# Layer 0 attention: the scores' 16-row tails ahead of the whole-array products

## The chip, the cores and the metric

The kernel runs on 1 core of one Trainium2 chip. The metric is device time in microseconds (us) of one execution.

## The reference

Two attention layers in sequence, all in float32, on an input of 2 images, 192 channels, 64 x 64 pixels (4096 tokens an image). Only layer 0 matters here:

```python
# --- layer 0 (conv_preact) ---
x = x + _L0_conv_ref(_gn(x), ...)
...
qkv = jnp.einsum('bchw,oc->bohw', x, w_qkv) + b_qkv[None, :, None, None]
qkv = lax.conv_general_dilated(qkv, w_dw, ..., feature_group_count=3 * c) + b_dw[None, :, None, None]
q, k, v = jnp.split(qkv, 3, axis=1)         # 4 heads of 48 channels
q = _l2norm(q, axis=2)
k = _l2norm(k, axis=2)
attn = jnp.einsum('bhdn,bhdm->bhnm', q, k) * temperature[None]
attn = jax.nn.softmax(attn, axis=-1)
out = jnp.einsum('bhnm,bhdm->bhdn', attn, v)
out = jnp.einsum('bchw,oc->bohw', out, w_proj) + b_proj[None, :, None, None]
```

Layer 1 is an attention of its own over the result (one head of 192 channels, 4096 tokens); it follows layer 0 in time and the change does not touch it.

## The kernel before, in words

Layer 0 (function `layer0`) treats 8 heads (4 heads x 2 images) one after the other. A head has 4096 queries and 4096 keys. Its scores are made transposed: a **step** n makes the scores of 128 keys (index m, 32 of them) against 1024 queries (index j, 4 blocks), so a head has 128 steps (`STEPS`) and the layer 1024. The five engines run programs of their own, coupled by semaphores.

What one step needs:

- **Scores, TensorE, lines 637 to 653** (`score`). Queries and keys are each split into a float16 high part and a float16 rest, and the product is high x high + high x rest + rest x high, a contraction over 3 x 48 = 144 rows. 128 of these are stacked in `q_a` and `k_a` and make a whole-array product (line 646), and the last 16 rows, the **tail**, stand in `q_b` and `k_b` and make a second product into the same sums (line 652). A step has two halves of 512 queries, so two whole-array products and two tails, in two PSUM banks. `q_b` and `k_b` hold the tail at the four partition starts 0, 32, 64 and 96, and the four tails of two steps sit in four different groups of 32 rows of the array. Two neighbouring steps have all four banks of `ps_s` between them (`ps_s[:, n % 2]`).
- **Exponential, ScalarE, line 437** (`head`): one instruction reads the 128 x 1024 scores and writes `prob`, of which there are four (`PR`). It waits for `scores` to count both halves of its step and for the weighing that read its `prob` tile last.
- **Weighing, TensorE, line 665** (`weigh`): `prob` (float32) times the values `vt`, whose 64 columns are put on the left or the right half of the array's columns, by half of the queries. The trace has four records for a step, as each float32 product stands there twice.

TensorE's program goes in **pairs of steps**: `score` for the two next steps, then `weigh` for the two steps before. `score` waits on `exped` before it writes into the bank of a step: the exponential of two steps earlier must have read it. The exponentials' semaphore starts at 2.

Behind some pairs the function `prep` puts other work of the next head: **projections** (line 574, float32, 96 x 112, four records each), **sums of squares** (line 588, into 32 columns, eight records) and **transposes** of the values (line 598, four records). In an even head 8 pairs are followed by a projection and two by a set of sums; in an odd head but the last 8 pairs by one projection, two by a set of sums, 4 by two projections each, and 8 by a set of transposes. There are four even heads and four odd heads. Their results go to `ps_h`, which has two banks, and VectorE or ScalarE empties it (VectorE lines 731, 755 and 800 to 802).

Each TensorE wait stands in the order of the program: what is behind it on TensorE waits too. Nothing but the order of the calls sets the order of work. VectorE (the depthwise convolution of the next head, norms, the end of each block), GpSimd and SyncE (the transfers) run beside it and are seldom waited for by TensorE.

Of the kernel before, what the change touches and what calls it, by code (L numbers as in the profile page):

```python
# [17 lines left out]
P = 128  # L18
HALF = 64
KR = HALF + HD  # L20
CH = 512
NCH = N // CH
KT = N // P
NB = 1024
# [8 lines left out]
TAIL = HD - REST  # L33
# [34 lines left out]
def layer0(nc, x, z_dram, w_qkv, vecs, temperature, consts, ss_dram, rn_dram, den_dram, o_dram):  # L68

    with ExitStack() as ctx:  # L70
        def sb(name, shape, dt=F32, scope=None):
            return (scope or ctx).enter_context(nc.sbuf_tensor(name, shape, dt))

        def psum(name, shape):
            return ctx.enter_context(nc.psum_tensor(name, shape, F32))

        def sem(name):
            return ctx.enter_context(nc.semaphore(name))
# [21 lines left out]
        q_a = sb("q_a", [P, 2, N], F16)  # L100
        k_a = sb("k_a", [P, 2, N], F16)
        q_b = sb("q_b", [P, 2, N // 2], F16)
# [37 lines left out]
        ps_s = psum("ps_s", [P, 2, NB])  # L140
# [21 lines left out]
        scores = sem("scores")  # L162
# [38 lines left out]
        with nc.Block() as block:  # L201
# [356 lines left out]
            def _(pe):  # L558
# [64 lines left out]
                for c in range(FAR, 8):  # L623
                    at = c - FAR
                    for tap in range(TAPS):
# [3 lines left out]
                                        start=(tap == 0), stop=(tap == TAPS - 1))  # L629
# [7 lines left out]
                def score(slot, g, a):  # L637
                    if a == 0:
                        for c in range(2):
                            pe.wait_ge(split_in[c], MOVES * 2 * (g + 1))  # L640
                    for n in (a, a + 1):
                        j, m = n // KT, n % KT
                        pe.wait_ge(exped, STEPS * g + n + 1)
                        for h in range(2):
                            cols = slice(j * NB + h * CH, j * NB + (h + 1) * CH)
                            pe.matmul(ps_s[:, n % 2, h * CH:(h + 1) * CH], k_a[:, slot, m * P:(m + 1) * P],  # L646
                                      q_a[:, slot, cols], start=True, stop=False)
                    for n in (a, a + 1):
                        j, m = n // KT, n % KT
                        for h in range(2):  # L650
                            r = REST * (2 * (n % 2) + h)
                            pe.matmul(ps_s[:, n % 2, h * CH:(h + 1) * CH], k_b[r:r + TAIL, slot, m * P:(m + 1) * P],  # L652
                                      q_b[r:r + TAIL, slot, j * CH:(j + 1) * CH], start=False, stop=True).then_inc(scores, 1)

                def head(slot, g, base, prep, pairs_moved=None, last=False):

                    uses = Uses(base)

                    def weigh(a):
                        j, m = a // KT, a % KT  # L660
                        pe.wait_ge(exped, STEPS * g + a + 3)
                        if m == 0:
                            pe.wait_ge(acc_free, NBL * g + j + 1)
                        for h in range(2):
                            ins = pe.matmul(ps_a[h * HALF:(h + 1) * HALF, j % 2, :], vt[:, slot, m, :],  # L665
                                            prob[:, a % PR, h * CH:(h + 1) * CH], start=(m == 0), stop=(m == KT - 1))
                        ins.then_inc(pv_done, 1)

                    for a in range(0, STEPS, 2):
                        if a + 2 < STEPS:  # L670
                            score(slot, g, a + 2)
                        elif not last:
                            score(1 - slot, g + 1, 0)
                        if a == 0:
                            pe.wait_ge(help_free, base)
                            if pairs_moved is not None:
                                pe.wait_ge(vt_moved, pairs_moved)
                        weigh(a)
                        weigh(a + 1)
                        for n in (a, a + 1):  # L680
                            j, m = n // KT, n % KT
                            prep(j, m, uses)
# [30 lines left out]

                pe.wait_ge(help_free, USE_FIRST)
                score(0, 0, 0)
                with pe.Fori(0, PAIRS - 1) as i:
                    even(i)
# [1340 lines left out]
```

## Time and profile before

| | us |
|---|---|
| median of 3 runs | 3410.62 |
| lowest and highest run | 3407.66, 3412.9 |
| the profiled execution, its own time | 3413.54 |
| its span | 3411.8 |
| TensorE matmul busy | 3197.9 (94%) |
| ScalarE busy | 2204.5 (65%) |
| VectorE busy | 1903.0 (56%) |
| GpSimd busy | 934.1 (27%) |

Times in the rows are microseconds from the start of the span, unless marked ns. PE is TensorE's matmul, PEld its weight load (which overlaps PE), ACT is ScalarE, DVE VectorE, POOL GpSimd, SP SyncE. A row of the timeline is a group of neighbouring instructions of one engine and line: start of the first, time from the first start to the last end, engine, line, operation, tiles written and read with their shapes, xcount, and in brackets the idle time of the engine ahead of it with what ended it. The end of a matmul is modelled by the profiler, so starts are the safer reading: a whole-array product of 512 columns is shown as 0.38 us long, while the next one starts 0.22 us after it. A window shows each group only with those of its instructions that touch the window, so a narrow window singles out one instruction.

### The profile page before, as it was taken

Reading aid. Unit: us, or ns where it says so; the run is one execution under the profiler, and the core shown is the slowest. Engines: PE = TensorE matmul, PEld = TensorE weight load, DVE = VectorE, ACT = ScalarE, POOL = GpSimd, SP = SyncE. Lnnn points to the kernel's source line nnn. Section 1 sums busy time; section 2 is a strip of 40 time slices with the busy share of each in tenths; the row PEclk is TensorE's granted clock in tenths of the full one; section 3 lists DMA queues with packets and bytes.
Section 4 is the critical chain, followed back from the end, with each engine's and each line's share of the span. In section 5 each row is a group of like instructions: output and inputs, shape, how many; then the busy total and the mean of one; then the engine's idle time right before and its main releaser. Section 6 shows DMA issues by size and latency. Waiting matters only on the chain. (4 is left out here: it accounts for less than half of the span.)

```text
span 3411.8 us, 47896 instructions
## 1 busy us (share of the span) xinstructions
PE 3197.9 (94%) x16354; PEld 1276.1 (37%) x16354; DVE 1903.0 (56%) x2461; ACT 2204.5 (65%) x2428; POOL 934.1 (27%) x485
## 2 busy tenths in 40 slices
PE   3799999999999999999999778999999787999998
PEld 1222222322223222222222234555555344555555
DVE  6551347431553525375111165888888555888886
ACT  5256556566555665565666524988888256888886
POOL 1002021020020210210200001666666213666665
PEclk7799999999999999999999979999999888999999
DMA  5312113111132021210200042677777824777777
GB/s 151 85 33 61 46 34 72 45 38 50 32 84 54 14 60 43 60 49 26 58 11 10 18 121 81 123 143 144 143 144 143 142 90 100 143 142 142 142 142 134
DMA packets 685382, 286.20 MB, mean 84 GB/s; under 512 B 602416, under 2 KB 644144, under 8 KB 682608
## 3 DMA queue, kind: packets, MB, share of 16 engines
q1 hardware_dynamic: 680400, 275.65, 38.0%
q10 hardware_dynamic: 4800, 8.26, 1.1%
q8 instruction: 97, 1.59, 0.2%
q14 instruction: 85, 0.70, 0.1%
HBM read 85.99 MB, written 34.21 MB: 35 GB/s over the span
## 5 line engine op out<-in xcount | busy, mean ns | idle before, releaser
L437 ACT ACTIVATE prob<-ps_s,cur 128x1024 f32<-128x1024 f32 x1024 | 1085.4, 1111 | 723.1 <-PE ps_s L652 722.0
L665 PE MATMUL ps_a<-prob,vt 128*64 128x512 f32 x4096 | 993.3, 606 | 0.0
L1623 PE MATMUL ps_s<-kst,qs 128*128 128x512 f16 x2560 | 640.4, 383 | 29.4 <-DMA qs<-q_scratch 18.8
L1319 POOL TENSOR_TENSOR p_lo<-gp,p_hi 128x1024 f16<-128x1024 f32 x256 | 550.6, 2161 | 399.6 <-ACT p_hi L1453 394.5
L1636 PE MATMUL ps_o<-v_hl,at_hi 128*128 128x384 f16 x2048 | 548.6, 329 | 33.6 <-DMA at_lo<-p_lo 33.3
L646 PE MATMUL ps_s<-q_a,k_a 128*128 128x512 f16 x2048 | 534.7, 383 | 4.2 <-issue 2.2
L1636 PE MATMUL ps_o<-v_hl,at_lo 128*128 128x192 f16 x2048 | 505.5, 248 | 0.0
L665 PEld LDWEIGHTS ps_a<-prob,vt 128*64 128x64 f32 x4096 | 248.7, 136 | 409.7 <-issue 409.0
L1890 DVE TENSOR_SCALAR_CACHE_REDUCE neg<-ps_s,mix 128x1024 f32<-128x1024 f32 x256 | 327.3, 1278 | 132.5 <-PE ps_s L1623 131.3
L1623 PEld LDWEIGHTS ps_s<-kst,qs 128*128 128x128 f16 x2560 | 245.1, 99 | 257.1 <-issue 31.4
L646 PEld LDWEIGHTS ps_s<-q_a,k_a 128*128 128x128 f16 x2048 | 132.5, 97 | 543.4 <-ACT prob L437 471.4
L405 POOL TENSOR_TENSOR sq<-qk 112x1024 f32<-112x1024 f32 x28 | 52.1, 1894 | 963.3 <-DVE qk L748 963.3
L1435 ACT ACTIVATE gp<-neg,nbias 128x1024 f32<-128x1024 f32 x256 | 290.1, 1133 | 0.0
L1636 PEld LDWEIGHTS ps_o<-v_hl,at_hi 128*128 128x128 f16 x2048 | 201.6, 98 | 201.2 <-DMA at_lo<-p_lo 44.9
L823 DVE RECIPROCAL rden<-rden 128x512 f32<-128x512 f32 x32 | 107.3, 3353 | 299.3 <-DMA rden<-den_scratch 299.3
L748 DVE SCALAR_TENSOR_TENSOR qk<-pad,vec,qk 112x2048 f32<-112x2048 f32 x112 | 254.0, 2346 | 0.0
L1636 PEld LDWEIGHTS ps_o<-v_hl,at_lo 128*128 128x128 f16 x2048 | 201.8, 99 | 51.1 <-issue 1.3
L1926 DVE SCALAR_TENSOR_TENSOR gp<-gp,coef,vb 128x1024 f32<-128x1024 f32 x128 | 209.2, 1675 | 7.2 <-DVE neg L1890 2.6
L1926 DVE SCALAR_TENSOR_TENSOR gp<-gp,coef,rn 128x1024 f32<-128x1024 f32 x128 | 207.5, 1663 | 5.8 <-DVE neg L1890 2.3
L731 DVE TENSOR_SCALAR pad<-ps_h,vec 112x512 f32<-112x512 f32 x80 | 60.1, 752 | 264.1 <-PE ps_h L574 264.0
L652 PE MATMUL ps_s<-q_b,k_b 16*128 16x512 f16 x2048 | 202.4, 385 | 0.0
L1419 ACT ACTIVATE vb<-neg 128x1024 f32<-128x1024 f32 x128 | 134.2, 1048 | 84.9 <-DVE neg L1890 84.7
(226 smaller groups left out, 2728.9 us busy)
## 6 DMA issues: line engine op xcount, KB each, us to landing
z<-z_scratch SPq DMA_DIRECT2D x80, 384.0 KB, 3.8
sq<-rn_scratch SPq DMA_DIRECT2D x14, 768.0 KB, 10.8
qs<-q_scratch SPq DMA_DIRECT2D x64, 128.0 KB, 2.8
rden<-den_scratch SPq DMA_DIRECT2D x64, 96.0 KB, 2.2
o_scratch<-o_s SPq DMA_DIRECT2D x64, 96.0 KB, 1.9
res_scratch<-xg SPq DMA_DIRECT2D x4, 1536.0 KB, 7.3
q_scratch<-qst SPq DMA_DIRECT2D x32, 192.0 KB, 2.4
res<-res_scratch SPq DMA_DIRECT2D x64, 96.0 KB, 2.2
```

The source lines that it names most:

```text
L437: act.activation(prob[:, a % PR, :], ps_s[:, a % 2, :], ACT.Exp, bias=cur[:, slot:slot + 1], scale=1.0 / SPLIT).then_inc(exped, 1)
L646: pe.matmul(ps_s[:, n % 2, h * CH:(h + 1) * CH], k_a[:, slot, m * P:(m + 1) * P], q_a[:, slot, cols], start=True, stop=False)
L652: pe.matmul(ps_s[:, n % 2, h * CH:(h + 1) * CH], k_b[r:r + TAIL, slot, m * P:(m + 1) * P], q_b[r:r + TAIL, slot, j * CH:(j + 1) * CH], sta ...
L665: ins = pe.matmul(ps_a[h * HALF:(h + 1) * HALF, j % 2, :], vt[:, slot, m, :], prob[:, a % PR, h * CH:(h + 1) * CH], start=(m == 0), stop=( ...
L748: ins = dve.scalar_tensor_tensor(out=out, in0=src, scalar=vec[0:KR, slot, 1 + tap:2 + tap], in1=out, op0=ALU.mult, op1=ALU.add)
L1319: pool.tensor_tensor(p_lo[:, cols], prob[s][:, cols], p_hi[:, cols], ALU.subtract).then_inc(lo_made[c], 1)
L1419: act.activation(sqr[s][:, cols], neg[:, c, :], ACT.Relu, scale=-1.0).then_inc(relued[c], 1)
L1435: act.activation(prob[s][:, c * QB:(c + 1) * QB], neg[:, c, :], ACT.Exp, bias=nbias[:, s, c:c + 1], scale=-1.0, accum_out=sums[:, s, c:c + ...
L1623: ins = pe.matmul(ps_s[:, c % 2, h * CH:(h + 1) * CH], qs[:, s, qt, :], kst[:, ktile, cols], start=(t == 0), stop=(t == len(terms) - 1))
L1636: ins = pe.matmul(ps_o[:, s * CH:s * CH + wide], a[:, s, kt, :], v_hl[:, kt, 0:wide], start=(kt == 0 and t == 0), stop=(kt == KT - 1 and t ...
L1890: dve.tensor_scalar(neg[:, c, :], ps_s[:, c % 2, :], mix[:, 6:7], None, ALU.mult, ALU.min, accum_out=nbias[:, s, c:c + 1]).then_inc(mx_op, 1)
L1926: dve.scalar_tensor_tensor(out=prob[s][:, cols], in0=prob[s][:, cols], scalar=coef[:, s, c:c + 1], in1=sqr[s][:, cols], op0=ALU.mult, op1= ...
```

## The change

In `score`, both waits on `exped` of the pair come first. Then come the four tails of the pair, which now begin the sums (`start=True`); then the four whole-array products, which complete them (`stop=True`) and each count up `scores`. Numbers of instructions, operands and the rest of the program stay. Lines behind 641 shift by one: the tails are at line 647, the whole-array products at 653, the weighing at 666, the projections stay at 574.

```diff
                     for n in (a, a + 1):
-                        j, m = n // KT, n % KT
                         pe.wait_ge(exped, STEPS * g + n + 1)
-                        for h in range(2):
-                            cols = slice(j * NB + h * CH, j * NB + (h + 1) * CH)
-                            pe.matmul(ps_s[:, n % 2, h * CH:(h + 1) * CH], k_a[:, slot, m * P:(m + 1) * P],
-                                      q_a[:, slot, cols], start=True, stop=False)
                     for n in (a, a + 1):
                         j, m = n // KT, n % KT
                         for h in range(2):
                             r = REST * (2 * (n % 2) + h)
                             pe.matmul(ps_s[:, n % 2, h * CH:(h + 1) * CH], k_b[r:r + TAIL, slot, m * P:(m + 1) * P],
-                                      q_b[r:r + TAIL, slot, j * CH:(j + 1) * CH], start=False, stop=True).then_inc(scores, 1)
+                                      q_b[r:r + TAIL, slot, j * CH:(j + 1) * CH], start=True, stop=False)
+                    for n in (a, a + 1):
+                        j, m = n // KT, n % KT
+                        for h in range(2):
+                            cols = slice(j * NB + h * CH, j * NB + (h + 1) * CH)
+                            pe.matmul(ps_s[:, n % 2, h * CH:(h + 1) * CH], k_a[:, slot, m * P:(m + 1) * P],
+                                      q_a[:, slot, cols], start=False, stop=True).then_inc(scores, 1)
```

TensorE, a regular pair near the start of the first even head, before (what an instruction waits for is in brackets; a float32 product is one row here):

```order
L643 REGISTER_ALU
L646 MATMUL ps_s<-q_a,k_a 128x512 [waits exped]
L646 MATMUL ps_s<-q_a,k_a 128x512
L643 REGISTER_ALU
L646 MATMUL ps_s<-q_a,k_a 128x512 [waits exped]
L646 MATMUL ps_s<-q_a,k_a 128x512
L652 MATMUL ps_s<-q_b,k_b 128x512 x4
L665 MATMUL ps_a<-prob,vt 64x512 [waits exped]
L665 MATMUL ps_a<-prob,vt 64x512
L665 MATMUL ps_a<-prob,vt 64x512 [waits exped]
L665 MATMUL ps_a<-prob,vt 64x512
```

The same pair now:

```order
L642 REGISTER_ALU
L642 REGISTER_ALU [waits exped]
L647 MATMUL ps_s<-q_b,k_b 128x512 [waits exped]
L647 MATMUL ps_s<-q_b,k_b 128x512 x3
L653 MATMUL ps_s<-q_a,k_a 128x512 x4
L666 MATMUL ps_a<-prob,vt 64x512 [waits exped]
L666 MATMUL ps_a<-prob,vt 64x512
L666 MATMUL ps_a<-prob,vt 64x512 [waits exped]
L666 MATMUL ps_a<-prob,vt 64x512
```

The tails moved from behind the whole-array products to ahead of them, and the second wait on `exped` from between the products to ahead of all.

TensorE, the end of a pair that a projection follows and the start of the next, in the same head, before:

```order
L665 MATMUL ps_a<-prob,vt 64x512 [waits exped]
L665 MATMUL ps_a<-prob,vt 64x512
L574 MATMUL ps_h<-z,w 112x512 [waits z_in1,help_free]
L574 MATMUL ps_h<-z,w 112x512
L643 REGISTER_ALU
L646 MATMUL ps_s<-q_a,k_a 128x512 [waits exped]
L646 MATMUL ps_s<-q_a,k_a 128x512
```

And now:

```order
L666 MATMUL ps_a<-prob,vt 64x512 [waits exped]
L666 MATMUL ps_a<-prob,vt 64x512
L574 MATMUL ps_h<-z,w 112x512 [waits z_in1,help_free]
L574 MATMUL ps_h<-z,w 112x512
L642 REGISTER_ALU
L642 REGISTER_ALU [waits exped]
L647 MATMUL ps_s<-q_b,k_b 128x512 [waits exped]
L647 MATMUL ps_s<-q_b,k_b 128x512 x3
```

Behind the projection's two products stood a whole-array product; now a tail stands there.

## Rows read from the trace of the kernel before

**Rows 1.** The page: TensorE's busy tenths in 40 slices of the span.

```profile
PE   3799999999999999999999778999999787999998
```

**Rows 2.** Windows by stage: attention of layer 0, layer 1.

```profile
core 0: us, PE busy (x) PEld busy (x) DVE busy (x) ACT busy (x) POOL busy (x), PEclk, DMA share, GB/s
145.00:1945.00 1800.00, 1794.40 (x8720) 494.33 (x8720) 705.05 (x533) 1085.43 (x1024) 210.24 (x63) 1.00 0.18 43
1945.00:3411.80 1466.80, 1328.93 (x7460) 750.23 (x7460) 1099.46 (x1820) 1060.19 (x1341) 715.08 (x406) 0.95 0.65 130
```

**Rows 3.** Timeline of one regular pair and the start of the next.

```profile
700.88 0.40 PE L652 MATMUL ps_s<-q_b,k_b 16*128 16x512 f16 x4
701.21 1.94 PE L665 MATMUL ps_a<-prob,vt 128*64 128x512 f32 x8
701.34 2.12 ACT L437 ACTIVATE prob<-ps_s,cur 128x1024 f32<-128x1024 f32 x2 [1.05 <-PE ps_s L652]
...
702.12 0.14 PEld L665 LDWEIGHTS ps_a<-prob,vt 128*64 128x64 f32 x2 [0.28 <-issue]
703.08 1.04 PE L646 MATMUL ps_s<-q_a,k_a 128*128 128x512 f16 x4
703.51 0.11 PEld L646 LDWEIGHTS ps_s<-q_a,k_a 128*128 128x128 f16 x2 [0.32 <-ACT prob L437]
704.05 0.10 PEld L652 LDWEIGHTS ps_s<-q_b,k_b 16*128 16x128 f16 x4 [0.42 <-issue]
704.05 0.39 PE L652 MATMUL ps_s<-q_b,k_b 16*128 16x512 f16 x4
```

**Rows 4.** Timeline, first and last start of a run of 98 regular pairs.

```profile
1629.10 0.39 PE L646 MATMUL ps_s<-q_a,k_a 128*128 128x512 f16 x1
...
1939.69 0.39 PE L646 MATMUL ps_s<-q_a,k_a 128*128 128x512 f16 x1
```

**Rows 5.** Timeline, a regular pair that follows transposes, start to next start.

```profile
609.45 1.03 PE L646 MATMUL ps_s<-q_a,k_a 128*128 128x512 f16 x4 [1.00 <-issue]
...
612.61 0.39 PE L646 MATMUL ps_s<-q_a,k_a 128*128 128x512 f16 x1
```

**Rows 6.** Timeline, the last whole-array product and last two weighing records of a pair.

```profile
700.57 0.38 PE L646 MATMUL ps_s<-q_a,k_a 128*128 128x512 f16 x1
...
702.55 0.60 PE L665 MATMUL ps_a<-prob,vt 128*64 128x512 f32 x2
```

**Rows 7.** Timeline in layer 1: a product's last part and its reader.

```profile
2201.20 0.38 PE L1623 MATMUL ps_s<-kst,qs 128*128 128x512 f16 x1
...
2201.62 1.28 DVE L1890 TENSOR_SCALAR_CACHE_REDUCE neg<-ps_s,mix 128x1024 f32<-128x1024 f32 x1 [0.59 <-PE ps_s L1623]
```

**Rows 8.** Timeline, pairs with a projection and with transposes.

```profile
184.93 1.03 PE L646 MATMUL ps_s<-q_a,k_a 128*128 128x512 f16 x4
...
187.55 0.60 PE L665 MATMUL ps_a<-prob,vt 128*64 128x512 f32 x2
188.08 1.97 PE L574 MATMUL ps_h<-z,w 96*112 96x512 f32 x4
...
189.46 0.59 PE L574 MATMUL ps_h<-z,w 96*112 96x512 f32 x1
189.89 1.03 PE L646 MATMUL ps_s<-q_a,k_a 128*128 128x512 f16 x4
...
604.25 0.60 PE L598 MATMUL ps_h<-ident,vv 112*128 112x112 f32 x4
604.59 0.26 PE L598 MATMUL ps_h<-ident,vv 112*128 112x112 f32 x1
604.68 0.38 PE L646 MATMUL ps_s<-q_a,k_a 128*128 128x512 f16 x1
...
607.84 0.60 PE L598 MATMUL ps_h<-ident,vv 112*128 112x112 f32 x4
```

**Rows 9.** Windows: eight pairs with transposes.

```profile
579.10:609.44 30.34, 29.00 (x162) 10.45 (x160) 10.62 (x21) 17.34 (x17) 0.00 (x0) 1.00 0.05 15
```

## The prediction

> **What bounds the kernel now.** I read the busy times by stage first. The change touches only the attention loop of layer 0, from 145 to 1945 us [rows 2]: TensorE is busy for 1794.4 of 1800 us at a granted clock of 1.00, that is 2.4 GHz, while ScalarE is busy for 1085 us. The page shows the same as a row of nines for PE [rows 1]. So a time can only change there by what TensorE's own sequence costs or by a wait put into it. Busy TensorE is modelled, however, so the order of starts has to be read.
>
> The timeline of one regular pair of steps [rows 3] gives it. Call the four whole-array products S, the four 16-row tails T, the value products V (eight records). Start to start: S to T 0.97, T to V 0.33, V to S 1.87, together 3.17 us. ScalarE in the same rows: two exponentials, 2.12 us, then 1.05 us idle until T has completed both score tiles. 2.12 + 1.05 is also 3.17. That is no accident: the third S's weights are loaded at 703.51, 0.05 us after the second exponential ends (701.34 + 2.12 = 703.46), 0.2 us later than they could be. Two rounds run side by side, TensorE's own and the one through ScalarE, and both last about 3.17 us.
>
> Which is longer? In a run of 98 regular pairs [rows 4] the period is (1939.69 - 1629.10)/98 = 3.169 us. A regular pair that follows other work, where the exponentials were long done, takes 612.61 - 609.45 = 3.16 [rows 5]. So the round through ScalarE binds by some 0.005 to 0.01 us, and TensorE's own round is the floor right below it.
>
> **What the change does to TensorE's own round.** The order S T V becomes T S V, with the same 16 records. What could change is the price of the boundaries. The last S starts at 700.57, T at 700.88 [rows 6]: 0.31, where one S follows another after 0.65/3 = 0.217 (four S busy 1.03, one 0.38 [rows 5, 6]). That is 0.095 extra. From the last V at 702.55 to S at 703.08 is 0.53, where V follows V after 0.43 (702.12 and 702.55, loads and products [rows 3, 6]): 0.10 extra. T to V is 0.33: T's 0.217, 0.01 over its four starts and 0.10. So each of the three changes of array shape costs nearly the same, and a regular pair has three of them in either order. The new round is then T to S 0.33, S to V 0.96 or 0.97, V to T 1.87: 3.165 us, as now without the ScalarE round.
>
> **What it does to the round through ScalarE.** Now the wait for the second exponential stands before T, and the first exponential needs only the first two S. From the end of the exponentials: 0.05 to T's load [rows 3], 0.33 to the first S, 0.23 to the second (rather than 0.217, as its load comes late after a boundary), and from that start to ScalarE's. A whole-array fp16 product releases its reader 0.42 after its start: 2201.20 to 2201.62 on VectorE [rows 7]. Tails need 0.45 (last of four at 700.89, ScalarE at 701.34 [rows 3]). Take 0.42, which is the same form of product: 0.05 + 0.33 + 0.23 + 0.42 + 2.12 = 3.15 us. This is 0.015 below TensorE's own 3.165, so TensorE binds alone. Per regular pair 3.169 falls to 3.165. There are 405 of them (511 pairs with both parts, less the 106 that carry other work, below): **-1.6 us**. Bounds: 3.16 gives -3.6, 3.17 gives +0.4.
>
> **The pairs with other work.** After V, 56 pairs hold one projection, 12 hold two, 24 hold a set of transposes and 14 a set of sums of squares (by the code: 32 + 24 single projections in even and odd heads, 12 double in three odd heads). Now a projection's last record at 189.46 is followed by S at 189.89 [rows 8]: 0.43, which is its own cadence, with no extra. A transpose at 604.59 is followed by S at 604.68, the same 0.09 us by which its predecessors follow each other, again no extra. These use the whole array in width, as S does, so nothing switches. V before the projection does pay: 187.55 to 188.08, 0.53. In the new order T follows the projection or transpose, so that boundary becomes one like S to T, and T to S adds the next. Such a pair goes from three priced boundaries to four. 92 pairs x 0.095 = **+8.7 us** (0.09 to 0.10: 8.3 to 9.2). Their S group also loses its smooth start (1.04 after a boundary [rows 3], 1.03 after a projection [rows 8]): 92 x 0.01 = **+0.9** (0 to 0.9). The 14 sums are 32 columns wide and pay on both sides either way: 0.
>
> No row of before has a projection followed by tails; the price above is taken from S to T. The Trainium skill, TensorEngine Tiling (Array Packing), Key Properties, says that changing the tiling mode, not just the tile, drains the engine. By it projection to S is free and projection to T is not, as in the sum, and it speaks against this change; rows 8 agree for the free half.
>
> Some of that is absorbed. Eight transpose pairs take 30.34 us [rows 9], 3.79 each, while an undisturbed one takes 607.84 - 604.25 = 3.59 [rows 8]; TensorE waits there for VectorE to empty the two helper banks. A longer boundary in front of such a wait shortens it. I take three pairs in each of three heads, 9 x 0.1 = **-0.9** (0 to -2.4, all 24).
>
> Nothing else moves. V's waits are for exponentials of the pair just awaited before T. Behind the merged wait stand S, V and the other work; S lost a head start of two products, which is what the floor of 3.165 counts. The ring of four prob tiles is freed by V of the pair before, done by then. VectorE, SyncE and GpSimd get the same instructions; layer 1 (1467 us) is untouched.
>
> **Sum:** 8.7 + 0.9 - 1.6 - 0.9 = +7.1 us, with ends +2.3 and +10.5. The profiled execution took 3413.54 us (span 3411.8), so 3420.6 by its own time; it lies 2.9 above the median of the runs, 3410.62, so the forecast is 3417.7. Its own range with the scatter of the runs (3407.66 to 3412.9) is 3411 to 3423. What a measurement of this kernel can tell from no change is about 0.2%, 6.8 us; the forecast sits on that edge.
>
> **Rivals.** (a) The round through ScalarE binds. It has only 0.015 us of room. Should a score tile be released as late as tails release it (0.45), it is 3.18; should T have to wait for its weight loads (0.10 for four [rows 3]) after the exponential, 3.25. Each 0.01 over 3.165 costs 4 us in 405 pairs: 3.18 to 3.25 is +6 to +34 on top, 3424 to 3452. Against: products start 0.01 after their load starts in all rows. Chance 0.13.
> On that release the Trainium skill, TensorE: Matmul & The Clock Gate (The cost: per-tile semaphore tail), states that increments of packed matmuls serialize at about 26 ns each. By it the whole-array products release earlier than the second tail did; rows 3 and 7 agree with 0.03 between 0.45 and 0.42, and it makes (a) less likely.
> (b) The other side: T to S costs no drain. This boundary is never seen in the trace. TensorE's round would be 3.07 and ScalarE's 3.05, so 405 x 0.10 = 40 us are gained, 14 sums pairs add 1, and the 92 pairs come out even: 3369. It decides as soon as the boundary costs under 0.07. Against: all three kinds of boundary seen cost 0.095 to 0.10. Chance 0.07. By the skill's rule on the tiling mode, above, it would not happen.
> (c) Projection to T costs nothing, as to S, because only V with its halves makes the array drain at that place. Then -1.6 and little else: 3409, no change. Against: S to T pays. Chance 0.08.
>
> **How the numbers follow.** The forecast has 0.72. Its centre, +7.1, is just over the bound of 6.8, so I give 0.38 of it to slower, 0.33 to no change and 0.01 to faster. With (a) slower, (c) no change, (b) faster: slower 0.51, same 0.41, faster 0.08. The range takes the forecast's own, (c), and the nearer part of (a), and leaves out (b) and the rest of (a): 3409 to 3430.
>
> **What would show it.** Right: V to T 0.53, T to S 0.31 from the last T, S to V 0.31; last projection record to T 0.53 instead of 0.43; periods in the 98-pair run 3.16 to 3.17; ScalarE idle some 1.04 per pair, its first exponential starting before the last S ends. Projection pairs 5.06 instead of 189.89 - 184.93 = 4.96 us [rows 8]. Wrong: V to T over 0.55 in regular pairs with ScalarE named as releaser (rival a), T to S 0.22 (b), projection to T 0.43 (c).

## The result, and the profile after

| | before | changed |
|---|---|---|
| median of the runs, us | 3410.7 (5 runs) | 3427.51 (5 runs) |
| lowest run, us | 3407.66 | 3425.66 |
| profiled execution: own time, us | 3413.54 | 3431.69 |
| its span, us | 3411.8 | 3429.9 |

One of the five runs of the changed kernel was disturbed (10419 us) and the ratio leaves it out; the median of the other four is 3426.93 us, 16.2 above the kernel before. The change makes the kernel slower: ratio 1.0048, 95% interval 1.0034 to 1.0062. The forecast was 3417.7 with a range of 3409 to 3430, and slower as the likeliest sign. The sign and the range hold; of the +16.2 us only +7.1 had been forecast.

The windows of the changed kernel, from its first to its last score product and over layer 1. The columns are those of [rows 2]:

```profile
143.99:1952.80 1808.81, 1804.49 (x8697) 524.41 (x8698) 704.51 (x531) 1082.39 (x1022) 210.11 (x63) 1.00 0.18 43
1957.20:3429.90 1472.70, 1335.75 (x7464) 751.15 (x7460) 1101.92 (x1820) 1060.64 (x1341) 713.31 (x406) 0.95 0.64 129
```

And of the kernel before, from its first to its last score product:

```profile
145.25:1939.69 1794.44, 1789.45 (x8696) 492.95 (x8696) 704.54 (x531) 1082.93 (x1022) 210.24 (x63) 1.00 0.18 43
```

The attention loop is 1808.8 - 1794.4 = 14.4 us longer, at the same granted clock of 1.00. Layer 1, whose program is the same, took between 1467 and 1473 us in the profiled executions of this study, so its difference here (1472.7 against 1466.8 [rows 2]) is the scatter of the measurement and not an effect.

Now the loop at rest. The timeline of a regular pair of the changed kernel in an even head, which answers to [rows 3] (tails are L647, products L653, weighing L666):

```profile
200.57 0.10 PEld L647 LDWEIGHTS ps_s<-q_b,k_b 16*128 16x128 f16 x4 [0.81 <-ACT prob L437]
200.58 0.40 PE L647 MATMUL ps_s<-q_b,k_b 16*128 16x512 f16 x4
200.91 1.04 PE L653 MATMUL ps_s<-q_a,k_a 128*128 128x512 f16 x4
201.55 2.12 ACT L437 ACTIVATE prob<-ps_s,cur 128x1024 f32<-128x1024 f32 x2 [1.04 <-PE ps_s L653]
201.87 1.94 PE L666 MATMUL ps_a<-prob,vt 128*64 128x512 f32 x8
203.74 0.10 PEld L647 LDWEIGHTS ps_s<-q_b,k_b 16*128 16x128 f16 x4 [0.81 <-ACT prob L437]
203.74 0.40 PE L647 MATMUL ps_s<-q_b,k_b 16*128 16x512 f16 x4
```

T to S 0.33, S to V 0.96, V to T 1.87: 3.16 us, as worked out. The exponentials end at 201.55 + 2.12 = 203.67, and the tails' weights are loaded at 203.74, 0.07 after that where a load that waits comes after 0.05: TensorE binds, with 0.02 us of room. Over a run of 25 such pairs it is (1038.73 - 959.62)/25 = 3.164:

```profile
959.62 0.40 PE L647 MATMUL ps_s<-q_b,k_b 16*128 16x512 f16 x4
...
1038.73 0.39 PE L647 MATMUL ps_s<-q_b,k_b 16*128 16x512 f16 x2
```

The pairs with a projection, which answer to [rows 8], last (194.25 - 184.12)/2 = 5.065 us in place of 4.96:

```profile
184.12 0.40 PE L647 MATMUL ps_s<-q_b,k_b 16*128 16x512 f16 x4
...
187.28 1.97 PE L574 MATMUL ps_h<-z,w 96*112 96x512 f32 x4
189.18 0.40 PE L647 MATMUL ps_s<-q_b,k_b 16*128 16x512 f16 x4
...
194.25 0.40 PE L647 MATMUL ps_s<-q_b,k_b 16*128 16x512 f16 x4
```

What was not forecast stands at the end of the loop. The same views of the changed kernel in the last two heads:

```profile
1649.47 2.12 ACT L437 ACTIVATE prob<-ps_s,cur 128x1024 f32<-128x1024 f32 x2 [1.12 <-PE ps_s L653]
1649.80 1.94 PE L666 MATMUL ps_a<-prob,vt 128*64 128x512 f32 x8
...
1651.14 0.60 PE L666 MATMUL ps_a<-prob,vt 128*64 128x512 f32 x2
1651.71 0.13 PEld L647 LDWEIGHTS ps_s<-q_b,k_b 16*128 16x128 f16 x4 [0.85 <-ACT prob L437]
1651.74 0.40 PE L647 MATMUL ps_s<-q_b,k_b 16*128 16x512 f16 x4
```

V to T (last two records at 1651.14, tails at 1651.74) is 0.60 in place of 0.53, and ScalarE is idle 1.12 in place of 1.04. The run of 98 pairs there, the counterpart of [rows 4], has (1952.80 - 1635.56)/98 = 3.237 us a pair:

```profile
1635.56 0.39 PE L647 MATMUL ps_s<-q_b,k_b 16*128 16x512 f16 x4
...
1952.80 0.40 PE L647 MATMUL ps_s<-q_b,k_b 16*128 16x512 f16 x4
```

Six of the eight heads run in a hardware loop (`pe.Fori`), the last two are written out behind it, as the kernel's `even(PAIRS - 1)` and `odd(PAIRS - 1, True)` say. What differs is in the view of the line that waits. For line 642 of the changed kernel it lists what TensorE's sequencer (PEldq) runs: operation, count, shortest, median and longest in ns, first and last start in us:

```profile
L642 PEldq ALU_OP  x759: 32/32/39, 146.8 to 1523.1; - x190
L642 PEldq EVENT_SEMAPHORE  x130: 51/51/51, 142.2 to 1952.7; - x130
```

Before, on its line 643:

```profile
L643 PEldq ALU_OP  x759: 32/32/39, 149.0 to 1519.4; - x190
L643 PEldq EVENT_SEMAPHORE  x2: 51/51/51, 143.7 to 1739.4; - x2
```

In the loop the number of a step is in a register, so each wait has a register instruction ahead of it (the last of the 759 is at 1523), and the first of the two waits rides on the second of these. In the last two heads the numbers are constants, there is no register instruction, and a pair's two waits meet in front of one weight load. There are 128 more instructions that only wait, 51 ns each. The same view for a narrow window shows the one of the pair above:

```profile
L642 PEldq EVENT_SEMAPHORE  x1: 51/51/51, 1651.6 to 1651.6; - x1
```

It starts at 1651.63 in the trace, 0.04 after the second exponential has ended (1651.59), and the tails' load comes 0.08 after that start. In 127 of the 130 the start is 0.04 after the end of the second exponential of a pair. So the later wait is the one that the separate instruction holds.

### The profile page after: what moved, and what is told of

Same layout as the page of the kernel before. It is cut to its first block and busy times, and to the rows that moved or that the text cites. A ratio compares the mean times of both kernels' runs of the same rounds, so it can differ in the third digit from the quotient of the medians.

```text
span 3429.9 us, 48023 instructions
## 1 busy us (share of the span) xinstructions
PE 3218.7 (94%) x16354; PEld 1308.3 (38%) x16354; DVE 1905.2 (56%) x2461; ACT 2204.0 (64%) x2428; POOL 932.2 (27%) x485
## 5 line engine op out<-in xcount | busy, mean ns | idle before, releaser
L666 PE MATMUL ps_a<-prob,vt 128*64 128x512 f32 x4096 | 993.5, 606 | 0.0
L653 PE MATMUL ps_s<-q_a,k_a 128*128 128x512 f16 x2048 | 532.9, 383 | 0.0
L666 PEld LDWEIGHTS ps_a<-prob,vt 128*64 128x64 f32 x4096 | 249.1, 136 | 510.4 <-issue 508.5
L653 PEld LDWEIGHTS ps_s<-q_a,k_a 128*128 128x128 f16 x2048 | 158.8, 98 | 237.7 <-issue 117.2
L647 PEld LDWEIGHTS ps_s<-q_b,k_b 16*128 16x128 f16 x2048 | 55.3, 91 | 407.0 <-ACT prob L437 334.3
L647 PE MATMUL ps_s<-q_b,k_b 16*128 16x512 f16 x2048 | 203.1, 385 | 4.5 <-ACT prob L437 1.9
```

## Experiments

Every version was timed beside the kernel before on the same chip; the ratios are to that kernel. Its medians beside them were 3413.1 us (one wait, waits apart, other work ahead, both edits), 3412.16 (old order with a doubled wait, with one wait, with the other work ahead of the weighing) and 3411.43 (old order with the other work between products and tails, and both edits once more). Two theories stood: **W**, that two waits in front of one instruction cost an instruction on the path from the exponential to the tails, in the last two heads; **D**, that each change of the array's shape costs 0.095 us. The rival to W was that the round through ScalarE is too long there for a reason of its own.

### One wait instead of two

```diff
-                    for n in (a, a + 1):
-                        pe.wait_ge(exped, STEPS * g + n + 1)
+                    pe.wait_ge(exped, STEPS * g + a + 2)
```

> The changed kernel, but the pair waits once on exped, for its second step; the first wait is implied by it. Theory W: in the last two heads, which are written out outside the loop, the two waits in front of the tails become an instruction of its own on TensorE (EVENT_SEMAPHORE L642 in the trace), and it puts 0.07 us into each of about 125 pairs. Then this version takes 3427.5 - 8.7 = 3419 us, V to T is 0.525 everywhere, and no semaphore row stands before the tails. Rival R: the round through ScalarE binds in those heads for a reason of its own (release, bank, ScalarE), whatever the form of the wait. Then it stays at 3427 us with V to T at 0.59 in the last two heads.

3419.35 us, ratio 1.0019 (1.0010 to 1.0028). The run of 98 pairs is back at (1943.84 - 1633.62)/98 = 3.165 us:

```profile
1633.62 0.39 PE L646 MATMUL ps_s<-q_b,k_b 16*128 16x512 f16 x3
...
1943.84 0.40 PE L646 MATMUL ps_s<-q_b,k_b 16*128 16x512 f16 x4
```

and the line that waits has two semaphore instructions left:

```profile
L641 PEldq EVENT_SEMAPHORE  x2: 51/51/51, 141.2 to 1744.3; - x2
```

W stands and the rival falls: ScalarE, the banks and the release are the same in this version. The loop, from its first to its last score product, is 1808.8 - 1801.0 = 7.8 us shorter than in the changed kernel; the ratios (1.0048 and 1.0019) are 0.0029 apart, some 10 us. It is also the kernel that the prediction had costed, and it is 6.2 us above the kernel before where the sum said 7.1.

### The two waits apart

```diff
-                    for n in (a, a + 1):
-                        pe.wait_ge(exped, STEPS * g + n + 1)
                     for n in (a, a + 1):
                         j, m = n // KT, n % KT
+                        pe.wait_ge(exped, STEPS * g + n + 1)
                         for h in range(2):
                             r = REST * (2 * (n % 2) + h)
```

> The changed kernel, with each wait in front of the two tails of its own step, so that no instruction carries two of them. Theory W: as with one wait, 3419 us, with V to T 0.525; the first two tails start early only where ScalarE is late, which is nowhere. Rival R: 3427 us. If the semaphore instruction came from the number of waits of the program, not from two on one instruction, it would be in this trace too.

3417.36 us, ratio 1.0014 (1.0005 to 1.0023). Both waits are there, each on the load of its own tails, and the semaphore instructions are 2 again:

```profile
L643 PEldq EVENT_SEMAPHORE  x2: 51/51/51, 142.5 to 1743.6; - x2
```

So it is not the number of waits but their meeting on one instruction.

### The kernel before with a doubled wait

```diff
                         j, m = n // KT, n % KT
+                        if not (isinstance(g, int) and g == 0 and n == 0):
+                            pe.wait_ge(exped, STEPS * g + n)
                         pe.wait_ge(exped, STEPS * g + n + 1)
                         for h in range(2):
                             cols = slice(j * NB + h * CH, j * NB + (h + 1) * CH)
```

> The kernel before, with a second, weaker wait on exped in front of each whole-array product group; nothing else. Theory W: in the loop the added wait rides on the register instruction and costs nothing; in the last two heads it is an instruction of its own behind the end of the second exponential, in front of the third product: 0.07 to 0.09 us in about 125 pairs, +9 to +11 us, 3420 us, the third product over 0.216 behind the second there. Rival R: the changed kernel's loss has to do with the tails coming first, and this version stays at 3411 us.

3420.46 us, ratio 1.0025 (1.0016 to 1.0034), 8.3 us above the kernel before. The price is paid with the tails last as well. The four products are 1.12 us from first start to last end in place of 1.04 [rows 3], since the third one's load comes late, and ScalarE is idle 1.12 in place of 1.05:

```profile
1641.14 1.12 PE L648 MATMUL ps_s<-q_a,k_a 128*128 128x512 f16 x4
1641.63 0.13 PEld L648 LDWEIGHTS ps_s<-q_a,k_a 128*128 128x128 f16 x2 [0.38 <-ACT prob L437]
...
1642.64 2.12 ACT L437 ACTIVATE prob<-ps_s,cur 128x1024 f32<-128x1024 f32 x2 [1.12 <-PE ps_s L654]
```

The exponentials ahead end at 1639.40 + 2.12 = 1641.52, so the load comes 0.11 after them where it came 0.05 after them before. Its semaphore line (L645 in this version) is:

```profile
L645 PEldq EVENT_SEMAPHORE  x256: 51/51/51, 140.8 to 1943.2; - x128
```

Half of these 256 stand ahead of the first product of a pair. Their exponential has ended some 0.6 us before that product's load, so they hold nothing up.

### The other work ahead of the weighing, in the new order

```diff
-                        weigh(a)
-                        weigh(a + 1)
                         for n in (a, a + 1):
                             j, m = n // KT, n % KT
                             prep(j, m, uses)
+                        weigh(a)
+                        weigh(a + 1)
```

> The changed kernel, both waits kept, but projections, sums and transposes stand between the scores and the weighing of their pair. Theory D (each change of the array's shape costs 0.095 us): 92 pairs go from four priced boundaries back to three, S to projection 0.22 or so without extra, projection to V 0.53: -8.7 to -9.6 us, 3418 us. Rival: the price belongs to work that follows V or precedes T whatever its shape; then it stays at 3427 us.

3415.06 us, ratio 1.0006 (0.9997 to 1.0015): some 14 us under the changed kernel by the two ratios (0.0042 x 3413), where 9.5 had been expected; the loops of the two traces are 13.8 us apart. The direction is D's; the size is explained by the trace of the version with both edits, below.

### The other work ahead of the weighing, in the old order

The same edit to the kernel before.

> The kernel before, with projections, sums and transposes between the scores and the weighing. Now they follow tails, so the 92 pairs have four priced boundaries in the old order: theory D expects the mirror image, +8.7 us, 3419.5 us, tails to projection about 0.31 and projection to V 0.53. Rival: if only the new order's tails after other work pay, it stays at 3411 us.

3419.22 us, ratio 1.0019 (1.0010 to 1.0029), 7.1 us above the kernel before. The mirror image came, and so the price is not one of the new order. A projection pair takes 192.56 - 187.49 = 5.07 us here too:

```profile
187.49 1.04 PE L646 MATMUL ps_s<-q_a,k_a 128*128 128x512 f16 x4
188.46 0.39 PE L652 MATMUL ps_s<-q_b,k_b 16*128 16x512 f16 x4
188.79 1.97 PE L574 MATMUL ps_h<-z,w 96*112 96x512 f32 x4
190.69 1.94 PE L665 MATMUL ps_a<-prob,vt 128*64 128x512 f32 x8
192.56 1.04 PE L646 MATMUL ps_s<-q_a,k_a 128*128 128x512 f16 x4
```

### Both edits: one wait, and the other work ahead, in the new order

> Both edits of the two runs above. Theories W and D add: 3427.5 - 8.7 - 9.5 = 3409 us, just under the kernel before (3410.7) by the 4 ns a pair that the round through ScalarE cost it. If either theory is wrong, 3418 or 3427 us.

3403.62 us, ratio 0.9972 (0.9960 to 0.9983): faster than both kernels. That is 9.5 us under the kernel before, where 2 had been expected. Its projection pair lasts 192.60 - 187.72 = 4.88 us:

```profile
187.72 0.40 PE L646 MATMUL ps_s<-q_b,k_b 16*128 16x512 f16 x4
188.04 1.04 PE L652 MATMUL ps_s<-q_a,k_a 128*128 128x512 f16 x4
188.92 1.88 PE L574 MATMUL ps_h<-z,w 96*112 96x512 f32 x4
190.73 1.94 PE L665 MATMUL ps_a<-prob,vt 128*64 128x512 f32 x8
192.60 0.39 PE L646 MATMUL ps_s<-q_b,k_b 16*128 16x512 f16 x4
```

Two things are gone from it. The projection follows the last product at once (188.04 to 188.92 is 0.88, four times the 0.22 at which the products follow each other). And its four records take 1.88 us, not the 1.97 of both kernels [rows 8]: behind products it lacks a delay of 0.09 inside, which it has behind the weighing and behind tails. So such a pair saves 0.18 us against the changed kernel, about twice what D alone gives; an undisturbed pair with transposes takes 3.55 in place of 3.70 us. Over 68 pairs with projections and 24 with transposes that is some 16 us. The version with one wait gained 16 (3419.35 to 3403.62); the changed kernel gained 14, and in its version two projections waited for their input `z`, 1.3 us together.

### The old order with the other work between products and tails

`score` takes the other work as a function and calls it between its two groups:

```diff
                             pe.matmul(ps_s[:, n % 2, h * CH:(h + 1) * CH], k_a[:, slot, m * P:(m + 1) * P],
                                       q_a[:, slot, cols], start=True, stop=False)
+                    if between:
+                        between()
                     for n in (a, a + 1):
```

> The old order (products, tails last), with projections, sums and transposes between the products and the tails. Which part of the gain of the version with one wait and the other work ahead of the weighing comes from the order of tails and products, and which from the place of the other work alone? Theory D: products to projection is free, projection to tails is paid, three priced boundaries as before; and the second half of a projection follows 0.43 behind the first in place of 0.52, as it does wherever a projection comes behind products. So V to S (0.53) + S (0.66) + 0.22 + 1.29 + 0.525 against 0.65 + 0.31 + 0.52 + 1.38 + 0.43: -0.08 us in each of 92 pairs, -7 us against the kernel before, regular pairs at 3.169 as before. If the gain came from the tails-first order: no change against before.

3409.3 us, ratio 0.9991 (0.9982 to 0.9999), 2.1 us under the kernel before where 7 had been expected. A projection pair came as worked out, 191.00 - 186.12 = 4.88 us, while an undisturbed one with transposes gained 0.04 only (3.55 in place of 3.59):

```profile
186.12 1.04 PE L646 MATMUL ps_s<-q_a,k_a 128*128 128x512 f16 x4
186.99 1.88 PE L574 MATMUL ps_h<-z,w 96*112 96x512 f32 x4
188.81 0.40 PE L654 MATMUL ps_s<-q_b,k_b 16*128 16x512 f16 x4
...
191.00 1.04 PE L646 MATMUL ps_s<-q_a,k_a 128*128 128x512 f16 x4
```

Some of the gain went into waits for input that the earlier projection met. Its waits on TensorE, with total, times and longest:

```profile
PE ps_h L574 <- DMA z<-z_scratch: 3.5, 2, 2.3
```

One of these two projections:

```profile
629.38 1.97 PE L574 MATMUL ps_h<-z,w 96*112 96x512 f32 x4 [1.23 <-DMA z<-z_scratch]
```

It stands behind whole-array products, with no change of the array's shape, and its four records still take 1.97 us and not 1.88. Whether these 3.5 us are in every execution was not tried.

The version with both edits was timed once more beside this one.

> The version with one wait and the other work ahead of the weighing once more, beside the run above on the same chip: 9 us below the kernel before, and 2 us below the run above (404 regular pairs at 3.164 in place of 3.169).

3404.07 us, ratio 0.9980 (0.9971 to 0.9988), 5.2 us under the run beside it, where 2 had been expected. Its trace has no wait of a projection for `z`, and between the two traces the 56 pairs with one projection make 278.2 - 273.5 = 4.7 of the 5.5 us by which the loops differ: in these two executions it is the waits for input just shown. The gain over the kernel before is 7.4 us here and 9.5 us in the run before.

### The old order with one wait ahead of the pair

```diff
+                    pe.wait_ge(exped, STEPS * g + a + 2)
                     for n in (a, a + 1):
                         j, m = n // KT, n % KT
-                        pe.wait_ge(exped, STEPS * g + n + 1)
                         for h in range(2):
                             cols = slice(j * NB + h * CH, j * NB + (h + 1) * CH)
```

> The kernel before (products first, tails last), but with one wait for the second exponential in front of the pair, as in the changed kernel. The round through ScalarE becomes 0.05 + 0.97 + 0.46 + 2.12 = 3.60 us in place of 3.17, in 404 regular pairs: +174 us, 3585 us. This prices what the tails-first order hides by releasing the first score tile from the middle of the products. If the wait were not what couples the two rounds: 3411 us.

3586.14 us, ratio 1.0514 (1.0498 to 1.0530), +174 us as worked out. The wait for the second exponential is thus what couples the two rounds, and the round can be read in its trace: exponentials from 1770.62 to 1772.74, products at 1772.80, tails at 1773.77, exponentials at 1774.22:

```profile
1770.62 2.12 ACT L437 ACTIVATE prob<-ps_s,cur 128x1024 f32<-128x1024 f32 x2 [1.48 <-PE ps_s L652]
...
1772.80 1.04 PE L646 MATMUL ps_s<-q_a,k_a 128*128 128x512 f16 x4 [0.37 <-ACT prob L437]
...
1773.77 0.39 PE L652 MATMUL ps_s<-q_b,k_b 16*128 16x512 f16 x4
...
1774.22 2.12 ACT L437 ACTIVATE prob<-ps_s,cur 128x1024 f32<-128x1024 f32 x2 [1.48 <-PE ps_s L652]
```

## Why the prediction was right, and where it was not

- **TensorE's own round, 3.165 us in either order.** Right: 3.164 over 25 pairs. The boundary that no trace had shown, tails to products, costs what the others do (0.33 from the first tail, 0.01 of it the four starts and 0.217 the stream), which rules out rival (b).
- **The round through ScalarE, 3.15 us.** Right in the loop: products release the exponential 0.42 after their start (the second starts at 201.13, ScalarE at 201.55), and 0.02 us of room is left. The regular pairs in the loop gain 0.005 us each. By the Trainium skill, TensorE: Matmul & The Clock Gate (The cost: per-tile semaphore tail), the increments of packed products are made one after the other. The trace agrees with that in its direction, 0.45 for the packed tails against 0.42; no run here separates the increments.
- **+8.7 and +0.9 for 92 pairs with a fourth boundary.** Right: 5.065 against 4.96 us for a projection pair. Rival (c) falls with it and with the mirror image in the old order. The Trainium skill, TensorEngine Tiling (Array Packing), Key Properties, says that a change of tiling mode drains the engine; the trace agrees at every boundary read, with 0.09 to 0.10 us each.
- **Absorbed at the transposes, -0.9.** Of the right kind. The loop's 14.4 us are 9.7 for the 92 pairs (0.105 each), 7.9 for some 116 regular pairs of the last two heads (3.237 - 3.169), -1.4 for the 288 in the loop (3.164 - 3.169); the remainder is -1.8. Summed from start to start, the 24 pairs with transposes went from 90.52 to 91.09 us, +0.6 where 24 x 0.105 = 2.5 was due: 1.9 was absorbed, twice the 0.9 of the sum and inside its bounds.
- **The step that failed** is "-1.6 us for 405 regular pairs" with "Nothing else moves". It priced all regular pairs alike, in the loop and behind it. In the 116 regular pairs of the last two heads the two waits share one instruction, and an instruction of 51 ns that only waits goes in between. The row count of the sequencer shows it (130 against 2), and one wait in place of two takes 8 us off. The prediction's own signs tell of it: it expected 3.16 to 3.17 in the run of 98 pairs, which has 3.237, and named V to T over 0.55 as a sign of being wrong, and it is 0.60 there. It is rival (a) in effect, the round through ScalarE bound at 3.237 us, but by a mechanism that the prediction didn't have: the way from the exponential's end to the load grew from the 0.05 of [rows 3] to 0.12 us (1649.47 + 2.12 = 1651.59, load at 1651.71), and the tails start 0.03 after it in place of 0.01. The sum lacked a term of 116 x 0.072 = +8.4 us. The Trainium skill, Perfetto Trace Analysis, Identifying Dependency Chains, says that instructions which wait on several engines may get separate semaphore instructions ahead of them. Here both waits were on one engine's one semaphore, and the trace still shows it.
- **The range held in part by luck.** 3427 us lies above the forecast's own 3411 to 3423. It is inside 3409 to 3430 because the range took in the nearer part of rival (a), whose two reasons, a late release and tails that wait for their weight loads, did not occur.

With the missing term the sum is 7.1 + 8.4 = 15.5 us, against 16.2 measured; the rest is within the scatter of layer 1.

From the exponential's end the way is 0.04 us to the separate instruction, 0.05 for it and 0.03 to the load. Why these pieces have these sizes is not shown.

## What to carry to other kernels

Where an engine waits right ahead of the work that another waits for, count the waits in front of one instruction: of two on the same rising semaphore the larger implies the other, and dropping the smaller took 8 us off here. Read a wait's price in each form in which the code is written out, in a loop with register numbers and in straight code with constants, since the one can hide what the other pays. And put work of one array shape beside work of the same shape: the order that looked neutral for a pair cost 0.1 us wherever it set a projection beside tails, and placing the projections and transposes beside the products took some 15 us off the version with one wait.

## What the runs showed of the hardware that was not expected

- Two waits on one semaphore in front of one weight load appear as an EVENT_SEMAPHORE of 51 ns, which starts 0.04 us after the later exponential has ended; the load follows 0.08 after its start, and a pair takes 3.237 us in place of 3.165. In the loop, where the wait rides on a register instruction of 32 ns, it costs nothing (3.164).
- A float32 projection of four records takes 1.97 us behind weighing or tails and 1.88 us behind whole-array products. The 0.09 us inside come on top of the 0.095 at the boundary. They do not need a change of shape: the six projections that waited for `z` right behind whole-array products, in three of the versions, take 1.97 us too. In these traces it is the projection behind a pause of TensorE that has them, whether the pause came from a change of shape or from a wait. What delays the later record was not tried.
